# Attention loop: the exponent taken twice from PSUM, row maxima at the head of the next step, projected chunks in a ring of four

## What is computed

```python
qkv = x @ W_qkv                      # 16 heads of 64
q, k = apply_rope(q), apply_rope(k)  # t * cos + rotate_half(t) * sin
dots = jnp.einsum('bhid,bhjd->bhij', q, k) * scale
dots = jnp.where(causal, neg, dots)
attn = jax.nn.softmax(dots, axis=-1)
out = jnp.einsum('bhij,bhjd->bhid', attn, v)
out = jax.nn.relu(out @ W_o1) @ W_o2  # then a layer norm
```

## Time and profile before

| | us |
|---|---|
| median of 3 runs | 5151.13 |
| the profiled execution | 5150.29 |
| its span | 5148.7 |
| busy PE, DVE, ACT, POOL over the span | 3708, 3685, 2558, 2348 |
| L2197 (subtraction), 640 times | 765.5 |
| L2224 (maxima) out of the peek buffer, 748 times | 667.3 |
| L2164 (exponent), 640 times | 631.7 |
| L2158 (f16 copy), 640 times | 588.1 |

### The profile page before, as it was taken

The page is one execution under the profiler, slowest core; times in us unless marked ns, Lnnn a source line. Parts: engine busy times, 40 slices in busy tenths (PEclk is TensorE's granted clock), DMA queues, the critical chain, the costliest instruction groups (busy, mean ns, idle before and its releaser), DMA issues. The chain is left out here.

```text
span 5148.7 us, 85718 instructions
## 1 busy us (share of the span) xinstructions
PE 3708.2 (72%) x28907; PEld 2589.2 (50%) x28907; DVE 3685.3 (72%) x4478; ACT 2557.9 (50%) x4164; POOL 2348.4 (46%) x1532
## 2 busy tenths in 40 slices
PE   2996645555555569849636898998888888885594
PEld 1663224444444446548613565565555555664483
DVE  6882589999999978820156887888878888875101
ACT  1222466666666622123113676777666666674121
POOL 0220278888888822120214655556656566600202
PEclk9998777777777789959858999999999999996697
DMA  2000001100101100026422222222222222202264
GB/s 84 0 0 5 6 23 31 31 29 29 31 29 31 29 22 0 20 84 193 132 88 57 54 53 47 47 49 69 52 63 52 51 52 55 52 4 90 79 192 132
DMA packets 237294, 276.27 MB, mean 54 GB/s; under 512 B 63771, under 2 KB 185556, under 8 KB 235536
## 3 DMA queue, kind: packets, MB, share of 16 engines
q1 hardware_dynamic: 224032, 244.85, 17.4%
q0 software_dynamic: 8704, 24.35, 1.4%
q10 hardware_dynamic: 4224, 2.76, 0.2%
HBM read 152.60 MB, written 36.04 MB: 37 GB/s over the span
## 5 line engine op out<-in xcount | busy, mean ns | idle before, releaser
L2197 DVE TENSOR_TENSOR att_b_prob_low<-att_b_prob,att_b_prob_high 128x1024 f16<-128x1024 f32 (+2 forms) x640 | 765.5, 1196 | 188.7 <-ACT att_b_prob_high L2158 156.3
L2164 ACT ACTIVATE att_b_prob<-att_b_score,att_soft 128x1024 f32<-128x1024 f32 (+2 forms) x640 | 631.7, 987 | 195.5 <-PE att_b_score L2069 121.5
L2224 DVE TENSOR_REDUCE att_b_neg_max<-att_b_peek 128x1 f32<-128x1024 f32 (+1 forms) x748 | 667.3, 906 | 71.5 <-PE att_b_peek L2046 55.4
L1037 PE MATMUL mix_scan_hT<-ident,mix_scan_h 128*128 128x128 f32 x1024 | 248.7, 390 | 535.1 <-DVE mix_scan_h L985 501.2
L2158 ACT CAST att_b_prob_high<-att_b_prob 128x1024 f16<-128x1024 f32 (+2 forms) x640 | 588.1, 919 | 32.8 <-PE att_b_o L2097 15.5
L2093 PE MATMUL att_b_o<-att_b_vh,att_b_prob_high 128*128 128x65 f16 x4352 | 462.8, 195 | 95.1 <-DVE att_b_heads L2215 54.7
L2093 PEld LDWEIGHTS att_b_o<-att_b_vh,att_b_prob_high 128*128 128x128 f16 x4352 | 399.2, 98 | 217.7 <-DVE att_b_prob_low L2197 129.3
L1037 PEld LDWEIGHTS mix_scan_hT<-ident,mix_scan_h 128*128 128x128 f32 x1024 | 172.1, 197 | 649.4 <-DVE mix_scan_h L985 443.8
L2095 PE MATMUL att_b_o<-att_b_vl,att_b_prob_high 128*128 128x64 f16 x4352 | 460.6, 193 | 0.0
L2097 PE MATMUL att_b_o<-att_b_vh,att_b_prob_low 128*128 128x65 f16 x4352 | 460.4, 194 | 0.0
L2067 PE MATMUL att_b_score<-att_b_q_both,att_b_k_twice 128*128 128x512 f16 (+3 forms) x1280 | 448.2, 350 | 8.9 <-issue 7.3
(11 more groups left out here) (339 smaller groups left out, 9526.5 us busy)
## 6 DMA issues: line engine op xcount, KB each, us to landing
moe_w<-in_L_ffn_W_dram SPq DMA_DIRECT2D x64, 1024.0 KB, 8.0
mix_scan_b_row<-mix_b_rows SPq DMA_DIRECT2D x128, 256.0 KB, 3.2
att_b_crossed<-att_b_raw SPq DMA_DIRECT2D x512, 64.0 KB, 2.0
att_b_q_both<-att_b_halves SPq DMA_DIRECT2D x240, 64.0 KB, 2.0
att_b_k_twice<-att_b_halves SPq DMA_DIRECT2D x240, 64.0 KB, 2.0
moe_slots_in<-moe_route_zero SPq DMA_DIRECT2D x2, 4096.0 KB, 14.3
moe_exp_x<-moe_slots_in SPq DMA_DIRECT2D x32, 256.0 KB, 4.3
moe_slots_out<-moe_exp_y POOLq DMA_DIRECT2D x32, 256.0 KB, 6.6
```

Of the source, the lines that this page charges most:

```text
L1037: last = pe.transpose(hT_ps[:, j * D + m * P:j * D + (m + 1) * P], hs[:, b * W + m * GRP + t * P:b * W + m * GRP + (t + 1) * P], ident[:, :])
L2164: act.activation(prob[:, at:at + width], score[m % 2][:, 0:width], ACT.Exp, scale=soft[:, 0:1])\
L2197: dve.tensor_tensor(prob_low[:, at:at + width], prob[:, at:at + width], prob_high[:, at:at + width], ALU.subtract).then_inc(low_ready, 1)
L2224: last = dve.tensor_reduce(neg_max[:, first + col:first + col + 1], peek_bank(kind, s)[:, base:base + nb * P], AX.X, ALU.max, negate=True)
```

## The change

The exponent of a piece is taken twice by ACT out of the same PSUM buffer, once in fp32 into `prob` and once in f16 into `prob_high`, directly after each other and before the side job; the copy `high_part` and its semaphore `high_ready` go, and `expd`, which frees the score buffer and lets DVE subtract, is raised by the second exponent. The second exponent also waits for `p_done`. On DVE the maximum of the slot peeked in step v is taken at the head of step v + 1, ahead of `low_part`, instead of in step v ahead of the side job; only in the turn `BEFORE` it stays. `raw` becomes a ring of four chunks: ACT's copy waits for the rotation of the chunk four back, and SP's `cross`, whose target `crossed` keeps a ring of two, now waits by itself for the rotation of the chunk two back.

```diff
+        RAWS = 4
-        raw, crossed = sb("raw", [P, 2 * GRP]), sb("crossed", [P, 2 * GRP])
+        raw, crossed = sb("raw", [P, RAWS * GRP]), sb("crossed", [P, 2 * GRP])
...
         def rotate(eng, c, t, i, kind):
-            ring = slice(r * GRP, (r + 1) * GRP)
+            ring, mine = slice(r * GRP, (r + 1) * GRP), slice(i % RAWS * GRP, (i % RAWS + 1) * GRP)
-            eng.tensor_tensor(raw[:, ring], raw[:, ring], cos[:, at], ALU.mult).then_inc(rope_step, 1)
+            eng.tensor_tensor(raw[:, mine], raw[:, mine], cos[:, at], ALU.mult).then_inc(rope_step, 1)
...
             def cross(t, i):
-                sp.wait_ge(raw_ready, qk_count(t + 1, i + 1))
+                copied, turned = qk_count(t + 1, i + 1), qk_count(t + 1, i - 1)
+                if not isinstance(t, int):
+                    copied, turned = sp.to_reg(copied), sp.to_reg(turned)
+                sp.wait_ge(raw_ready, copied)
+                wait_unless_first(sp, roped, turned)
...
         ACT, turn:
-                    if has_piece(kind, v - 1):
-                        high_part(t, v - 1)
                     if has_piece(kind, v):
                         exponents(t, v)
...
         ACT, side:
-                    r = i % 2
+                    r = i % RAWS
-                    wait_unless_first(act, roped, qk_count(p, i - 1))
+                    wait_unless_first(act, roped, qk_count(p, i - RAWS + 1))
...
-            def high_part(t, m):
-                at, width = m % 2 * SPAN, width_of(m)
-                act.wait_ge(expd, piece(t, m + 1))
-                wait_unless_first(act, p_done, piece(t, m - 1))
-                act.copy(prob_high[:, at:at + width], prob[:, at:at + width]).then_inc(high_ready, 1)
             def exponents(t, m):
-                act.activation(prob[:, at:at + width], score[m % 2][:, 0:width], ACT.Exp, scale=soft[:, 0:1])\
+                act.activation(prob[:, at:at + width], score[m % 2][:, 0:width], ACT.Exp, scale=soft[:, 0:1])
+                wait_unless_first(act, p_done, piece(t, m - 1))
+                act.activation(prob_high[:, at:at + width], score[m % 2][:, 0:width], ACT.Exp, scale=soft[:, 0:1])\
                     .then_inc(expd, 1)
...
         DVE, turn:
+                    peek_at = slot_at(kind, v if kind == BEFORE else v - 1)
+                    if peek_at and not (kind == FIRST and v == 0):
+                        maximum(t, kind, *peek_at)
                     if has_piece(kind, v - 1):
                         low_part(t, v - 1)
                     if v >= 2 and has_piece(kind, v - 2) or v < 2 and has_piece(kind, -1):
                         take(t, b, v - 2)
-                    peek_at = slot_at(kind, v)
-                    if peek_at:
-                        maximum(t, kind, *peek_at)
...
             def low_part(t, m):
-                dve.wait_ge(high_ready, piece(t, m + 1))
+                dve.wait_ge(expd, piece(t, m + 1))
```

More of the change, by code:

```diff
@@ L1779, in attention_heads @@
         w_loaded, tables, x_loaded, acc_stored, acc_cleared, wo_loaded, masks, unit_rows, w_step, w_split, qk_projected, raw_ready, rope_step, roped, v_projected, v_high, \
-            v_ready, peeked, maxed, min_ready, min_turned, row_ready, scored, expd, high_ready, low_ready, p_done, \
+            v_ready, peeked, maxed, min_ready, min_turned, row_ready, scored, expd, low_ready, p_done, \
             inv_ready, o_taken, h_turned, hT_ready, o_ready, added = map(sem, (
@@ L1783, in attention_heads @@
                 "roped", "v_projected", "v_high", "v_ready", "peeked", "maxed", "min_ready", "min_turned", "row_ready",
-                "scored", "expd", "high_ready", "low_ready", "p_done", "inv_ready", "o_taken", "h_turned", "hT_ready",
+                "scored", "expd", "low_ready", "p_done", "inv_ready", "o_taken", "h_turned", "hT_ready",
                 "o_ready", "added"))
@@ L1815, in rotate @@
             eng.wait_ge(crossed_over[r], crossed_count(p, i))
-            eng.tensor_tensor(raw[:, ring], raw[:, ring], cos[:, at], ALU.mult).then_inc(rope_step, 1)
+            eng.tensor_tensor(raw[:, mine], raw[:, mine], cos[:, at], ALU.mult).then_inc(rope_step, 1)
             c.n += 1
             c.link(eng.tensor_tensor(crossed[:, ring], crossed[:, ring], sin[:, at], ALU.mult))
-            c.link(eng.tensor_tensor(raw[:, ring], raw[:, ring], crossed[:, ring], ALU.add), (tables, 32))
+            c.link(eng.tensor_tensor(raw[:, mine], raw[:, mine], crossed[:, ring], ALU.add), (tables, 32))
             if kind != BEFORE or i >= 2:
                 wait_apart(eng, stacked[r], stacked_count(p, i), (tables, 32))
-            c.link(eng.tensor_scalar(high(r), raw[:, ring], 1.0, None, ALU.mult))
-            eng.tensor_tensor(low16(r), raw[:, ring], high(r), ALU.subtract).then_inc(roped, 1)
+            c.link(eng.tensor_scalar(high(r), raw[:, mine], 1.0, None, ALU.mult))
+            eng.tensor_tensor(low16(r), raw[:, mine], high(r), ALU.subtract).then_inc(roped, 1)
             assert c.n == ROPE_STEPS
@@ L1899, in cross @@
             def cross(t, i):
-                ring = slice(i % 2 * GRP, (i % 2 + 1) * GRP)
-                sp.wait_ge(raw_ready, qk_count(t + 1, i + 1))
+                ring, mine = slice(i % 2 * GRP, (i % 2 + 1) * GRP), slice(i % RAWS * GRP, (i % RAWS + 1) * GRP)
+                copied, turned = qk_count(t + 1, i + 1), qk_count(t + 1, i - 1)
[3 more added lines that the diff above has]
+                wait_unless_first(sp, roped, turned)
                 for to, fro in ((0, 32), (32, 0), (64, 96), (96, 64)):
-                    sp.dma_start(crossed[to:to + 32, ring], raw[fro:fro + 32, ring])\
+                    sp.dma_start(crossed[to:to + 32, ring], raw[fro:fro + 32, mine])\
                         .then_inc(crossed_over[i % 2], 16)
```

## The result

The changed kernel takes 5224.16 us (median of 4 runs, 5223.5 to 5225.71) against 5150.96 us before: ratio 1.0147, 95% interval 1.0132 to 1.0162, 73 us slower. Forecast were 5235 us and 84 us slower. The profiled execution took 5225.71 us, 75.4 us more than the one before, in a span of 5224.1 us.

A forecast was written before the change was run, and what follows sets the result against it. POOL's rope chain was taken to bound steps 0 to 21, DVE the rest. Per turn +3.9 + 2.5 - 0.8 = +5.6 us; 15 turns, +84 us on 5151, gave 5235 us, range 5178 to 5278 (chance 0.50).

The forecast's parts named there:

- What bounds what: Attention's pairs loop: POOL's rope chain bounds steps 0 to 21 of a turn, DVE bounds steps 22 to 39.
- Block 1: Steps 0 to 21 of a turn, 66.1 us in the sample before; forecast to gain 0.8 us.
- The exponent twice: Both exponents before ACT's side copy: nearly all of DVE's 156.3 us of idling goes, 0.8 us gained a turn.
- the nearest row: First turn's POOL chain, without gaps: 53.8 us against a mean of 54.4, taken as 0.8 us gained a turn.
- block 3: Steps 28 to 39 of a turn: 33.4 us instead of 30.9, +2.5.
- the bank: Score buffer held one exponent longer: forecast to cost nothing; as a rival 96 us more, about 5331 us, chance 0.04.
- the gaps give nothing back: POOL's chain in steps 0 to 21 gains nothing: +6.4 us a turn, 5247 us; rival's chance 0.20, shared with another.
- The swap on DVE: Maximum behind the side job, DVE idles for PE's side matmuls: +3.9 us in steps 22 to 27, +2.5 in 28 to 39.
- block 2: Steps 22 to 27 of a turn: 23.5 us, against a mean of 19.6 before, +3.9.
- Step 22: DVE idles from PE's peek to the correction: 3.9 us, or 2.6 if the granted clock stays up.
- The granted clock: PE's longer wait at step 22 (8 us) lowers its clock: 1.3 us a turn, granted below 1.00 behind it.
- The ring of four: Four raw chunks let ACT copy further ahead in steps 0 to 21: zero time.

The follow-up runs named there:

- copy_in_place: Changed kernel with the f16 copy back in place of the second exponent, the first exponent freeing the score bank: 5228.39 us, ratio 1.0157 to the kernel before.
- ring2: Changed kernel with a ring of two instead of four for the projected chunks: 5217.81 us, ratio 1.0137 to the kernel before.
- rope_short: One POOL rope instruction cut from 512 to 32 columns, in the changed kernel (ratio 0.9976) and in exp_only (0.9750), both to the kernel before.
- lead23: exp_only with the peeks 23 instead of 24 steps ahead, two mrow jobs and one out job moved a step: 5105.26 us, ratio 0.9896 to the kernel before.
- exp_only: Changed kernel with DVE's old order (maximum ahead of the side job), second exponent and ring of four kept: 5133.81 us, ratio 0.9978 to the kernel before.
- swap_out_only: Changed kernel with the maximum ahead of the side job again in steps 22, 23, 24 and 28 only: 5174.12 us, ratio 1.0069 to the kernel before.
- max_only: Kernel before with only DVE's order changed (maximum at the head of the next step): 5240.98 us, ratio 1.0176.
- warm_after: Changed kernel with 24 overwritten matmuls issued by PE before its wait for the keys in step 22: 5211.58 us, ratio 1.0103 to the kernel before.
- rope_short_after: Changed kernel with POOL's second rope instruction cut from 512 to 32 columns, so attention values differ: 5145.91 us, ratio 0.9976 to the kernel before.

## Why the prediction was right

*What bounds what.* Right. Block 1 ends 5.2 to 5.4 us behind POOL's sixth chunk in every turn of the changed kernel, copy_in_place, ring2, both rope_short kernels and lead23, and in all but one turn of exp_only and of swap_out_only and three of max_only. Shortening POOL's work shortens it (rope_short_*).

*The exponent twice.* Forecast: DVE's waits for ACT go, block 1 gains 0.8 us between bounds of 0 and 3.3, as POOL stays last. Measured: 66.3 to 65.5 us, 0.8. Within it the chain itself fell by 1.2 us (54.3 to 53.2, the gaps between its chunks from 2.9 to 0.1) and its start came 0.4 later. So POOL's instructions did stretch into most of what the gaps gave, as the nearest row had it. But that the size agrees is in part luck: the exponent alone (exp_only) takes the gaps to 0.4 us, and there the chain falls by only 0.4 (to 54.0) and block 1 by 0.1. The rest came only with the swap beside it, and why is not shown. What the exponent alone gives, 1.2 us a turn, is in block 3 (-1.3), for which the prediction named no gain. The cost of the second exponent on ACT, at most 43 us of its time, was hidden, and so was the bank: copy_in_place.

The prediction also weighed a rule of the Trainium skill (page SBUF — State Buffer, section Who interferes with whom: the shared ports are an exclusive lock, and the loser blocks fully). The trace agrees with the rule. In the changed kernel POOL's L1824, 1.16 us alone, began 23 times while a subtraction of 1024 columns (and no second one) had 0.4 us or more to go, and took 1.48 to 2.00 us; each time it ended 1.01 to 1.02 us after the subtraction, however long it had run beside it. Once it began first, by 0.03 us: it took its 1.16 us, and the subtraction 2.20 (timeline of the changed kernel, DVE and POOL):

```profile
3306.76 1.21 DVE L2196 TENSOR_TENSOR att_b_prob_low<-att_b_prob,att_b_prob_high 128x1024 f16<-128x1024 f32 x1
3307.13 1.85 POOL L1824 TENSOR_TENSOR att_b_halves<-att_b_raw,att_b_halves 128x512 f16<-128x512 f32 x1
...
2812.35 1.16 POOL L1824 TENSOR_TENSOR att_b_halves<-att_b_raw,att_b_halves 128x512 f16<-128x512 f32 x1
2812.38 2.20 DVE L2196 TENSOR_TENSOR att_b_prob_low<-att_b_prob,att_b_prob_high 128x1024 f16<-128x1024 f32 x1 [0.23 <-ACT att_b_prob_high L2163]
```

What the prediction drew from the rule, that the gaps give nothing back (5247 us), came out in part: of 2.9 us of gaps 1.2 came back in the changed kernel, 0.4 in exp_only. Which of the two engines starts first decides who is stretched, so the rule by itself does not fix that sum.

*The swap on DVE.* Forecast +3.9 us in block 2 and +2.5 in block 3; measured, with the exponent's share in them, +3.9 (20.3 to 24.2) and +2.2 (31.6 to 33.8). Against exp_only the swap costs 3.6 and 3.4 us and gives 0.7 back in block 1: 6.4 a turn, the forecast total of 3.9 + 2.5, but shared out otherwise. By steps: DVE's idling was put at 1.5 us in steps 24 and 28 and is 1.37 and 1.53; at 1.2 in step 26 and is 1.43; at 0.5 each, one of them at 0.7, in steps 30, 31, 37 and 38 and is 0.92, 0.57, 0.73 and 0.38. Step 22, put at 3.9 us from peek to correction, takes 4.19 in the sample. Step 23 was missed: 0.9 us of idling were forecast and there are 0.15, as the subtraction ahead took 1.99 us instead of 1.21. Block 2 came out at 23.5 us all the same, with more busy time (16.3 for 15.5) and less idle time (7.2 for 8.0). The order of the queue alone makes the loss: max_only.

*The granted clock.* Forecast: PE's longer wait costs 1.3 us in step 22. It waited 6.2 us on average, less than the 8 assumed; warm_after gives back 0.44%, 1.5 us a turn (1.3 by the traces, all of it in block 2).

*The ring of four.* Forecast zero; ring2 agrees.

*The sum.* 5.6 us a turn were forecast, 5.2 measured. 15 x 5.2 = 78 us, where the two profiled executions differ by 75.4; the rest of the program gave 3 back. Of the 11 us between 5235 and 5224, 15 x 0.4 = 6 are the turns, mostly block 3, 3 the rest of the program, and 2 the difference between the profiled executions and the medians. The mechanism of the loss is right; that the sum agrees so closely owes something to shares that cancel. Of the signs named, one was put too sharply: PE's wait is over 6 us in 12 of the 15 turns, but 3.7 to 4.3 in three. The turn was put at 121 to 123 us: the sample takes 121.6, the mean of the 15 is 123.5.

## What to carry to other kernels

Where a wait ends at a constant distance behind one engine's instruction in every repetition, however long the waiter stood, that engine's chain is likely the bound, and shortening it, as rope_short_after does, shows it, even if it is busy less than half of the span; removing other waits ahead of it mostly lengthens this one, and the way to use such slack is to move the point of use. On an engine that works in order, an instruction that is ready belongs ahead of one that waits for another engine: exchanging them costs the uncovered part of that wait in every repetition. And a longer wait of PE had a second price behind it here, in the clock that it is granted.

## What was not expected of the hardware

PE, kept busy with 5.3 us of useless matmuls inside a wait of 7 us, was granted its full clock (1.00 against 0.58 in the 4 us behind the wait), and the kernel was 0.4% faster for it (in lead23 matmuls of this kind held the clock in only seven of 15 turns, with no gain that can be told). Two exponents of the same 128x1024 PSUM buffer back to back start 1.00 us apart on ACT though each is recorded with 1.11 (the f16 copy out of SBUF took 1.05):

```profile
3303.01 1.11 ACT L2161 ACTIVATE att_b_prob<-att_b_score,att_soft 128x1024 f32<-128x1024 f32 x1
3304.01 1.12 ACT L2163 ACTIVATE att_b_prob_high<-att_b_score,att_soft 128x1024 f16<-128x1024 f32 x1
```
